# Two edge layers of a graph network on one core: joint signals for TensorE's folds and row sums, and small sums between gathers

## What is computed

```python
# second layer: one of 8 edge types picks a 16x16 matrix
A = edge_emb[edge_type].reshape(-1, 16, 16)
msg = jnp.einsum('emh,eh->em', A, features[edge_src])
m = jax.ops.segment_sum(msg, edge_dst, num_segments=6250)      # then a GRU step
# fourth (last) layer: one of 90 relations, and a scalar per edge
W_rel = jnp.matmul(w_comp, weight.reshape(16, 30, 16)).reshape(90, 16, 16)
e = jnp.concatenate([h[src] @ Ws.T, he @ Ws.T, h[dst] @ Ws.T], axis=1) @ Wa.T
msg = jnp.einsum('ei,eio->eo', h[src], W_rel[rel_type]) * e
h_out = jax.ops.segment_sum(msg, dst, num_segments=6250)
```

## Time and profile before

| | us |
|---|---|
| median of three runs | 4394.57 |
| lowest and highest run | 4373.16, 4407.93 |
| the profiled execution | 4357.18 |
| its span, first to last instruction | 4353.5 |
| PE busy in the span | 3665.5 (84%) |
| DVE busy | 2710.6 (62%) |
| POOL busy | 1900.8 (44%) |
| ACT busy | 1324.1 (30%) |
| mean granted clock of PE over the span | 0.882 |

### The profile page before, as it was taken

How to read it: one execution, slowest core, us unless ns; L and a number is a source line. 1 busy time by engine, 2 the same in 40 slices (tenths; PEclk the granted TensorE clock), 3 DMA queues, 4 the chain that set the end, 5 groups by cost and what they waited for, 6 DMA issues and landing times. The chain is left out here.

```text
span 4353.5 us, 77864 instructions
## 1 busy us (share of the span) xinstructions
PE 3665.5 (84%) x28548; PEld 2130.3 (49%) x28548; DVE 2710.6 (62%) x6415; ACT 1324.1 (30%) x2874; POOL 1900.8 (44%) x1856
## 2 busy tenths in 40 slices
PE   6787879999998768888889896672799989998998
PEld 4566645544554324444444443341455555555555
DVE  8999953222212546676666674442677767777777
ACT  6999930011000213332333331340122212222222
POOL 1000006830000466676667650267366666666650
PEclk8999989998999879898888997665799888888889
DMA  5444468662465412222222225771122222222221
GB/s 149 83 83 80 60 270 304 219 236 91 168 238 245 138 30 50 50 51 47 44 50 51 51 51 192 295 238 18 37 44 44 44 39 44 46 45 41 44 44 40
DMA packets 471195, 445.62 MB, mean 102 GB/s; under 512 B 357553, under 2 KB 406609, under 8 KB 459675
## 3 DMA queue, kind: packets, MB, share of 16 engines
q1 hardware_dynamic: 389178, 391.82, 29.1%
q0 software_dynamic: 55216, 38.70, 6.0%
q10 hardware_dynamic: 26417, 10.05, 0.9%
HBM read 346.18 MB, written 95.85 MB: 102 GB/s over the span
## 5 line engine op out<-in xcount | busy, mean ns | idle before, releaser
L1814 POOL DMA_INDIRECT rows<-typed_table,ring x640 | 754.4, 1179 | 368.1 <-issue 180.1
L2225 PE MATMUL l_ps_g<-ring,h_part 128*128 128x512 f16 x2660 | 641.8, 401 | 92.3 <-issue 81.3
L1408 PE MATMUL L_ps<-ring,L_T 128*128 128x448 fp8e4 (+1 forms) x4606 | 670.9, 382 | 45.6 <-DMA ring<-adj 42.1
L2191 POOL DMA_INDIRECT ring<-typed_table,l_idxA x384 | 397.1, 1034 | 275.8 <-PE l_ps_x L2312 163.9
L1408 PEld LDWEIGHTS L_ps<-ring,L_T 128*128 128x128 f16 (+1 forms) x4606 | 327.9, 104 | 375.8 <-issue 60.8
L2191 POOL DMA_INDIRECT l_rows<-typed_table,l_idxA x384 | 394.6, 1028 | 234.1 <-PE l_ps_x L2312 127.4
L2231 ACT ACTIVATE l_sel<-l_ps_g 128x512 f16<-128x512 f32 x380 | 226.1, 597 | 851.6 <-PE l_ps_g L2225 399.1
L2225 PEld LDWEIGHTS l_ps_g<-ring,h_part 128*128 128x128 f16 x2660 | 273.6, 103 | 431.4 <-issue 165.4
L620 PE MATMUL cells<-keys,lows 128*128 128x147 f16 (+5 forms) x2744 | 372.6, 283 | 121.6 <-DVE keys L581 105.9
L2206 DVE TENSOR_SCALAR ring<-l_krow,W 128x1024 f16<-128x1024 f16 x570 | 234.7, 483 | 302.9 <-remote 183.2
L2260 PE MATMUL l_ps_w<-rel,l_tyh 90*128 90x256 bf16 x2544 | 397.5, 327 | 19.1 <-DVE ring L2288 15.6
(11 more groups left out here) (369 smaller groups left out, 4466.4 us busy)
## 6 DMA issues: line engine op xcount, KB each, us to landing
ring<-adj SPq DMA_DIRECT2D x67, 2744.0 KB, 10.9
adj<-ring SPq DMA_DIRECT2D x14, 2744.0 KB, 9.1
typed_table<-ring SPq DMA_DIRECT2D x49, 765.0 KB
ring_fifth<-src_div_mod_rows SPq DMA_DIRECT2D x122, 256.0 KB
l_krow<-src_div_mod_rows SPq DMA_DIRECT2D x95, 256.0 KB
l_trow<-type_row SPq DMA_DIRECT2D x106, 180.0 KB
attr<-in_he POOLq DMA_DIRECT2D x25, 512.0 KB, 5.7
klast<-last_keys SPq DMA_DIRECT2D x81, 128.0 KB
```

Source lines behind the costliest of these rows:

```text
L1408: ins = pe.matmul(bank[at:at + rows, 0:CH], d["T"][q][:, k, 0:rows], ring[r][:, k, :], start=n < side, stop=n >= NT - side, tile_position= ...
L1814: r_tok_[g] = r_in[b].by(pool.indirect_dma_start(rows[b][:, j, :], None, t1_dram, bass.IndirectOffsetOnAxis(ap=idxA[:, k * SUP + j:k * SUP ...
L2191: rt_tok[g] = r_in[b].by(pool.indirect_dma_start(table_rows[b][:, j, 0:RC], None, t3_dram, bass.IndirectOffsetOnAxis(ap=idxA[:, k * SUP + ...
L2225: ins = pe.matmul(ps_g[p][:, 0:HE], parts[p][:, j, :], hot[b][:, j, h * HE:(h + 1) * HE], start=j == 0, stop=j == GJ - 1)
```

## The change

In `typed_layer` the fold's last matmul gives no signal any more. Its token is that of the first half of the next gather, and `keep_rows` is called inside `gather`, ahead of the copies of the first half. The row sums move ahead of `message`, and the last of them has no signal: the message's does for both. In `relation_layer` a half of a gather gives one signal instead of two, and both copies follow it. The sums by target of the messages stand between the two halves, under the second half's signal; the sums of the table rows stand behind the second half, under the signal of the next iteration's first half of `expand`. `expand` is called in two halves with the fold (and a tile of the table, in the plain part) between them; the fold's token is the signal of the second half, and a half gives one signal.

```diff
@@ typed_layer, gather
                     gat[i, h] = c_gat.by(ins)
+                    if i and h == 0:
+                        fold_tok[i - 1] = gat[i, h]
+                        keep_rows(i - 1)
                     act.wait_ge(*gat[i, h])
-                    if i >= 2 and h == 0:
-                        act.wait_ge(*fold_tok[i - 2])
...
@@ fold_rows
-                fold_tok[i] = c_fold.by(ins)
+                if i + 1 == n:
+                    fold_tok[i] = c_fold.by(ins)
@@ sum_types
                 if i:
+                    sum_rows_behind(i - 1)
                     message(i - 1)
...
@@ message
                 m_tok[i] = c_m.by(pe.matmul(ps_m[at, 0:F], byt[i % 2][:, :], w("emb_out"), start=True, stop=True, tile_position=(0, i % 2 * WIN)))
+                for g in after[i][-1:]:
+                    a_tok[g] = m_tok[i]
+
+            def sum_rows_behind(i):
+                for g in after[i]:
+                    ins = row_sums(g)
+                    if g != after[i][-1]:
+                        a_tok[g] = c_a.by(ins)
+                        keep_sums(GK[g], a_tok[g])
+                        store_sums(GK[g])
@@ row_sums
-                a_tok[g] = c_a.by(ins)
+                return ins
@@ the loop
                     fold_rows(i - 1)
-                    keep_rows(i - 1)
...
+                if i < n:
+                    gather(i)
+                if i == n:
+                    keep_rows(n - 1)
                 if 1 <= i <= n:
                     make_typed(i - 1)
-                if i < n:
-                    gather(i)
...
-                    for g in after[i - 3]:
-                        row_sums(g)
+                    for g in after[i - 3][-1:]:
                         keep_sums(GK[g], a_tok[g])
                         store_sums(GK[g])
@@ relation_layer, gather
-                    gat[i, h] = c_gat.by(ins)
-                    act.wait_ge(*gat[i, h])
-                    if p == 0 and i >= 2 and by_matmul[i - 2]:
-                        act.wait_ge(*fold_tok[i - 2])
+                gat[i, h] = c_gat.by(ins)
+                act.wait_ge(*gat[i, h])
+                if i >= 2 and by_matmul[i - 2]:
+                    act.wait_ge(*fold_tok[i - 2])
+                for p in range(2):
                     selt[p, "sel"] = selt[i, h] = c_sel.by(act.activation(sel[b][2 * h + p][:, :], ps_g[p][:, 0:HE], ACT.Relu))
@@ expand
-            def expand(i, between=()):
+            def expand(i, half):
                 pe.wait_ge(*ty_tok[i])
-                for q in range(SUP // 2):
-                    if q == SUP // 4:
-                        for m in between:
-                            table_tile(m)
+                for q in range(half * SUP // 4, (half + 1) * SUP // 4):
...
-                    if q % 2:
-                        w_tok[i, q - 1] = w_tok[i, q] = c_w.by(ins)
+                w_tok[i, q - 1] = w_tok[i, q] = c_w.by(ins)
+                if half == 1 and by_matmul[i]:
+                    fold_tok[i] = w_tok[i, q]
@@ add_up
-                a_tok[k] = c_a.by(ins)
+                return ins
@@ the loop
                 if 1 <= i <= n:
+                    expand(i - 1, 0)
+                    for k in unsignalled:
+                        a_tok[k] = w_tok[i - 1, 0]
+                        put_sums(k)
+                    unsignalled = []
                     if by_matmul[i - 1]:
                         fold_rows(i - 1)
+                    for m in tiles[ahead:ahead + 1]:
+                        table_tile(m)
+                    expand(i - 1, 1)
+                    if by_matmul[i - 1]:
                         keep_rows(i - 1)
-                    expand(i - 1, tiles[ahead:ahead + 1])
...
-                if i < n and by_matmul[i]:
+                gathers = i < n and by_matmul[i]
+                if gathers:
                     gather(i, 0)
+                if i >= 2:
+                    k = EK[i - 2]
+                    summed = add_up(k, dstP[(i - 2) % 3], msg[(i - 2) % 3], 2 * F, msg_tok[i - 2], dst_tok[i - 2])
+                if gathers:
                     gather(i, 1)
                 if i >= 2:
-                    k = EK[i - 2]
-                    add_up(k, dstP[(i - 2) % 3], msg[(i - 2) % 3], 2 * F, msg_tok[i - 2], dst_tok[i - 2])
+                    a_tok[k] = gat[i, 1] if gathers else c_a.by(summed)
                     put_sums(k)
                     for g in after[i - 2]:
                         k = GK[g]
-                        add_up(k, dstG[g % 4], table_rows[g % RT], MC, rows_tok[g], dstg_tok[g])
-                        put_sums(k)
+                        summed = add_up(k, dstG[g % 4], table_rows[g % RT], MC, rows_tok[g], dstg_tok[g])
+                        if i < n:
+                            unsignalled.append(k)
+                        else:
+                            a_tok[k] = c_a.by(summed)
+                            put_sums(k)
```

4 lines of the change are left out of this document (3 added, 1 removed).

## The result

The changed kernel took 4401.7 us (median of 20 runs, 4359.7 to 4446.1) against 4374.7 for the one before (20 runs, 4335.1 to 4413.8): a ratio of 1.0076, 95% interval 1.0047 to 1.0104. The ratio leaves out the slow runs of either kernel, those over 1.5% above its fastest; the medians without them are 4401.0 and 4367.7. So it is a little slower, within the 1% band, where 4340 was forecast. Its profiled execution took 4387.34 us, with a span of 4383.0 (before 4353.5).

What follows compares the result with a forecast made beforehand. PE was taken as the bound, its last-layer iterations stretched by late instructions and a lowered clock. 55 us off for the pause and 0 for the rest gave 4394.6 - 55 = 4340 us, range 4215 to 4425.

Steps and rivals of the forecast that it cites:

- the pause: Last layer: PE's idle waits and low clock shrink, from 13.57 to 12.91 us an iteration, 55 us over 83 iterations.
- Added switches: Last layer: a second pair of switches between gathers and small sums per iteration, +0.19 us, 17 us if PE never waits.
- Signals worth 0: Last layer: 4 signals an iteration in place of 9 save PE nothing; a skill's rule would estimate 12 us.
- Just covered: Last layer: signal and ACT's later copy, 0.4 and 0.6 us, fit behind 1.1 us of small sums.
- G in the last layer, DVE's 0.39 us: Last layer: G 0.4 to 0.6 us later, just met by DVE's idleness and PE's longer iteration: 0, else 18 us.
- The part of the first edge layer: First edge layer: row sums' order, joint signal and G taken 2.6 us later are together worth 0 us.
- The price given for a late G, 24 us: First edge layer: 0.2 us of DVE delay times 122, 24 us, only if it were on the path.
- A: Rival, 0.28: in the last layer waits only move, the clock still falls every second iteration, only switches count: 4395 to 4412.
- C: Rival, 0.12: DVE becomes the last layer's bound through late G; 40 to 80 us plus 17 of switches: 4450 to 4490.
- B: Rival, 0.15: last layer's waits go for good, as signals and instructions share a way into PE; about 175 us: 4220.
- What would show it: Signs: last layer's clock 0.95 or more, iterations near 12.9 us, quiet end 11.1; first edge layer unchanged within 10 us.

Runs made afterwards that it cites:

- runs 4 to 6: Kernel before with, in the last layer, one move: messages' sums between gather halves (1.0041); fold between expand halves (1.0006); both sums groups between gather halves (1.0147).
- run 7: Kernel before with a signal on every small matmul of the last layer that had none, 29 more an iteration; ratio 0.9998.
- run 3: Kernel before with the change's last-layer part alone, but a signal and a copy per gather group as before; ratio 1.0029.
- runs 12 and 13: Second layer fetches one tile of table rows in place of eight: in the kernel before (0.9858), and with the change's fold edit in that layer (0.9886).
- typed_fold: Kernel before with only the second layer's fold edit: no signal on the fold, G behind the next gather half; ratio 1.0145.

## Why the prediction was right or wrong

- **"I take that: 13.57 - 12.91 = 0.66 us, times 83 = 55 us" for the pause.** This step failed, and with it the sign. Waits did not shrink: iterations went from 13.78 to 14.54 us, PE's idleness from 1.11 to 1.63 us in each, and the clock only from 0.89 to 0.90. The argument counted large matmuls as cover for late instructions, and ahead of the small sums the idleness did fall, from 43.7 to 14.6 us. But the lateness sits in the signals too, and the change puts more behind each signal: idleness went to the gather's second half (34.6 us more, up to 5.9 at a time), to the folds (21.9 more) and to the expansion (12.0 more). The trace shows what PE waits for there, ACT's copies and "issue"; that the joint signals are the cause is argued, since no part of the change ran where signals are late. The 12.91 us of the earlier trace rows belonged to a quieter stretch of the old order; nothing in the trace said that the new order would have more such stretches. The subtraction itself started from one pair's mean, 13.57, and not from the stretch's 13.78, which would have given 72 us.
- **"Added switches ... +0.19 us."** Right in kind, too small: a second block of sums costs 0.43 us (runs 4 to 6). What was missed is that the two groups of sums, placed apart, take 2 x 1.05 us against 1.78 together. It was also taken as hidden where PE waits; if every iteration pays it, it is 36 of the 63 us lost in 83 iterations. That it is paid in full is seen in the 25 iterations of 11.38 us and the quiet end, not in the others.
- **Signals worth 0.** Right, shown with 29 more of them (run 7). It should have weighed more: with the signals worth nothing the change had no sure gain at all, only sure costs. The run shows this where signals come in time.
- **"Just covered", ACT's copies behind a joint signal.** Right where signals are in time (the quiet end; run 3). On the first chip this is the place of the long waits.
- **G in the last layer, DVE's 0.39 us.** DVE keeps 0.18 us of idleness in the quiet end, at an iteration longer by 0.43. It does not become the bound there. With POOL at work it did stand longer before the product with G, 75.9 us in 81 iterations against 20.8 in 83.
- **"The part of the first edge layer ... 0 us".** Wrong on the later chips, by 54 to 59 us of layer and 1.0 to 1.45% of time, all of it from the late G. The DVE part of the step was right: the product starts later, and nobody on PE's side waits for it (runs 12 and 13). The step did not follow the third engine. There POOL is busy without a pause, and what lengthens its instructions moves the rows. The price given for a late G, 24 us, was under half of it. On the first chip, for which the step was written, it is not refuted: POOL stood 160.1 us for free buffers, so longer fetches had room, and the layer was 31 us shorter in the one execution that was profiled; why is open.
- **Rivals.** A's time (4395 to 4412) holds the result, but its mechanism, "only the switches count", is half of it at best, and its sign, iterations still alternating between 12.8 and 14.3 us, is gone. For the other half C had the chain that the trace shows, late signals with no second part to hide ACT's copy, but it made DVE the bound where PE stands for the copies, and its price was higher: 0.33 us an iteration, 27 us, where 40 to 80 were given. B did not come: with 4 signals in place of 9 the iterations grew.
- **What would show it.** Of the forecast's numbers none came: iterations near 12.9 us, clock at 0.95, quiet end at 11.1. PE's idleness did spread, but 57.7 of 131.7 us stand ahead of the gather, which was not named. The first edge layer was to be unchanged within 10 us and was 31 us shorter. What was named for C, DVE idle for over 1 us before the product with G in most iterations, is there in part: 26 of 81, where before had 6 of 83.

Open is how the parts share the 1.0076 on the first chip, since no part was run there. The profiled executions say -31 and +67 us for the layers, which is one execution each. That the time lies inside the stated range owes something to luck: the second layer's 31 us, for which the prediction had 0, take back half of what the last layer lost.

## What to carry to other kernels

A signal that is taken from a later instruction makes its consumer late even when the giver pays nothing, so follow not only who waits for the consumer but which other engine its timing disturbs, and ask whether that engine is the one that has no pause. Small matmuls among large ones were paid by the block here: keep the blocks together, and put something between a gather and the work that needs its copy. Where VectorE's long instructions with two SBUF inputs run beside GpSimd's indirect DMAs and GpSimd has no pause, try halving them: on the later chips that alone took 1% off the kernel.

## What the runs showed of the hardware

- The same program takes 4375 us in the first comparison and 3778 to 3783 us on the three later chips, with a granted clock of 0.84 and 0.98 in the last layer. In the slower case signals reach other engines late while POOL issues indirect DMAs or just behind it: the gathers that ended at 4219.14 were followed by ACT's copies only at 4224.82. After the wait of 5.38 us that this gave PE, its granted clock is 0.68 for 7.5 us, and 1.00 again behind it. Why the cases differ was not found.
- POOL's indirect DMA takes 0.94 us beside an idle VectorE. One that starts 0.06 to 1.05 us into a product of VectorE with two SBUF inputs ends 0.81 to 0.83 us behind the product's end (116 of 116 in typed_fold), so it takes up to 1.99 us; the product keeps its 1.22 us, also where the fetch started up to 0.15 us before it. With products of half the width the mean falls from 1.28 to 1.08 us.
- 29 more signals in an iteration of 10.95 us cost nothing.
- A block of 16 small f32 passes among large f16 matmuls takes 1.05 us from its start to the next, two groups together 1.78 us.
